# Layer 1 attention: when the row-score products stand among the transposed ones, and where the first row terms are sent

## The reference

```
q = (x @ W_query).reshape(b, n, NUM_HEADS, HEAD_DIM).transpose(0, 2, 1, 3)
k = (x @ W_key).reshape(...)   # v likewise
scores = jnp.einsum('bhqd,bhkd->bhqk', q, k)
scores = jnp.where(causal, -jnp.inf, scores)
attn = jax.nn.softmax(scores / jnp.sqrt(jnp.float32(HEAD_DIM)), axis=-1)
ctx = jnp.einsum('bhqk,bhkd->bhqd', attn, v)
```

## Time and profile before

| | |
|---|---|
| median of three runs | 1362.34 us (1362.08 to 1362.48) |
| profiled execution, its own time | 1362.70 us |
| its span, first to last instruction | 1361.0 us |
| PE busy | 1243.6 us (91%) |
| DVE busy | 812.6 us (60%) |
| ACT busy | 589.7 us (43%) |
| mean granted TensorE clock | 0.962 |
| the stage of layer 1's tiles (first exponential to last) | 808.05 to 1058.64 us |

### The profile page before, as it was taken

One profiled execution on the slowest core, in us unless ns is written; L12 is line 12 of the kernel. 1 busy time (PEld: TensorE's weight loads), 2 busy tenths in 40 slices (PEclk: granted clock), 3 DMA queues, 4 the chain that ended last, 5 costly groups with the idle time before them and its releaser, 6 DMA issues. The chain is left out here.

```text
span 1361.0 us, 18268 instructions
## 1 busy us (share of the span) xinstructions
PE 1243.6 (91%) x5944; PEld 859.5 (63%) x5944; DVE 812.6 (60%) x1732; ACT 589.7 (43%) x1091; POOL 470.8 (35%) x335
## 2 busy tenths in 40 slices
PE   6999999999999999999998968889997478999887
PEld 6866878888887788888885512223322247778665
DVE  6467754444444344444456767777775556878565
ACT  2322633333333333333334425766777153433553
POOL 3101445555555555555563221111111033312000
PEclk9999899999999999999999969999999788999899
DMA  4100253333332643333421350232200301110001
GB/s 152 41 20 1 82 147 109 108 108 108 108 108 54 160 111 108 108 108 108 108 70 47 128 159 22 77 79 70 70 17 17 87 0 47 34 48 24 1 15 47
DMA packets 49308, 102.67 MB, mean 75 GB/s; under 512 B 8660, under 2 KB 21716, under 8 KB 49244
## 3 DMA queue, kind: packets, MB, share of 16 engines
q1 hardware_dynamic: 49244, 101.87, 26.6%
HBM read 88.52 MB, written 8.93 MB: 72 GB/s over the span
## 5 line engine op out<-in xcount | busy, mean ns | idle before, releaser
L473 DVE TENSOR_TENSOR q_t<-q_t,ps 128x512 f32<-128x512 f32 x132 | 90.8, 688 | 230.3 <-ACT q_t L416 227.7
L1554 DVE CUSTOM_DVE_ANT_0 masked<-ps,causal 128x128 f32<-128x128 f32 (+7 forms) x256 | 184.4, 755 | 55.9 <-PE ps L1375 55.1
L529 POOL TENSOR_TENSOR wqkv<-q_t,v_tok 128x512 f32<-128x512 f32 x132 | 198.0, 1516 | 25.9 <-DVE q_t L473 15.2
L519 POOL TENSOR_TENSOR d_w_lo<-raw,d_w_hi 128x768 fp32r<-128x768 f32 x66 | 122.7, 1860 | 242.8 <-ACT d_w_hi L389 242.8
L465 DVE TENSOR_TENSOR wqkv_lo<-wqkv,wqkv_hi 128x512 fp32r<-128x512 f32 x132 | 155.0, 1174 | 67.9 <-ACT wqkv_hi L395 67.9
L311 PE MATMUL ps<-h_hi,d_w_hi 128*128 128x512 f32 x528 | 167.2, 397 | 1.9 <-POOL d_w_lo L519 1.0
L311 PE MATMUL ps<-h_hi,d_w_lo 128*128 128x512 f32 x528 | 166.0, 395 | 0.0
L311 PE MATMUL ps<-h_lo,d_w_hi 128*128 128x512 f32 x528 | 166.0, 395 | 0.0
L1534 ACT ACTIVATE xn<-ps 128x512 f32<-128x512 f32 (+3 forms) x256 | 117.3, 512 | 58.1 <-PE ps L1395 56.3
L389 ACT CAST d_w_hi<-raw 128x768 fp32r<-128x768 f32 x66 | 55.0, 833 | 195.1 <-PE ps L324 193.5
L311 PEld LDWEIGHTS ps<-h_hi,d_w_hi 128*128 128x128 f32 x528 | 98.9, 189 | 25.8 <-POOL d_w_lo L519 1.9
(11 more groups left out here) (252 smaller groups left out, 2119.1 us busy)
## 6 DMA issues: line engine op xcount, KB each, us to landing
v_tok<-router_weights_t SPq DMA_DIRECT2D x132, 256.0 KB, 3.8
raw<-in_moe SPq DMA_DIRECT2D x66, 384.0 KB, 4.3
qk<-qk_parts SPq DMA_DIRECT2D x72, 128.0 KB, 2.7
qk_parts<-parts SPq DMA_DIRECT2D x16, 384.0 KB, 2.7
raw<-in_mlp SPq DMA_DIRECT2D x16, 384.0 KB, 3.1
h_t<-qk_parts SPq DMA_DIRECT2D x24, 128.0 KB, 2.8
x_tok<-in_x SPq DMA_DIRECT2D x4, 512.0 KB, 8.2
h_hi<-raw SPq DMA_DIRECT2D x32, 64.0 KB, 2.3
```

Source lines behind the costliest of these rows:

```text
L473: nc.vector.tensor_tensor(prod[:, s % 3, :], sg[:, s % 3, :], ps[:, 2 * (s % 2) + 1, :], ALU.mult).then_inc(s_t, 1)
L519: nc.gpsimd.tensor_tensor(w_lo[:, slot, :], raw[:, slot, :], w_hi[:, slot, :].bitcast(F32), ALU.subtract).then_inc(s_wlo, 1)
L529: nc.gpsimd.tensor_tensor(inter[:, s % 3, :], prod[:, s % 3, :], wbc[:, s // 2, (s % 2) * GW:(s % 2 + 1) * GW], ALU.mult).then_inc(s_int, 1)
L1554: nc.vector.tensor_tensor_reduce(masked[:, at % 2, 0:k], ps[:, bank:bank + 2, :].rearrange("p a n -> p (a n)")[:, 0:k], causal[:, SEQ - k: ...
```

## The change

Two things are changed; no instruction is added or taken away, and both are changes of order. First, `due` is computed from columns: an item counts its columns and 256 more, a tile likewise, and the list of items is advanced in proportion to the columns of tiles done, between goals at the group ends (R of the group, plus EARLY, plus LEAD). Second, `rows(0)` moves ahead of `load_qk(sp, 2)` and the two loads behind it.

```
-                due = [min(len(entries), ahead + (at * 3 + min(h, 2) + 1) * (HQ * TB + 1) // (3 * NTI)
-                           + min(LEAD, at * LEAD // NTI)) for at in range(NV * NTI) for h in range(HQ)]
+                def columns(n):
+
+                    return (n % TB + 1) * P + 2 * P if n < HQ * TB else 2 * P
+
+                filled = [0] + list(itertools.accumulate(columns(n) for _, n in entries))
+                spent = [0] + list(itertools.accumulate(
+                    (4 * g + 4 - max(4 * g, j)) * P + 2 * P for g, j in tiles for h in range(HQ - 1)))
+
+                def target(v, steps):
+
+                    goal = lambda u, lead: filled[min(len(entries), place[min(u, NV - 1), HQ * TB] + 1 + EARLY + lead)]
+                    a, b = goal(v, LEAD if v else 0), goal(v + 1, LEAD)
+                    return a + (b - a) * spent[steps] // spent[-1]
+
+                due = [sum(c <= target(v, n * (HQ - 1) + min(h, HQ - 2) + 1) for c in filled[1:])
+                       for v in range(NV) for n in range(NTI) for h in range(HQ)]
...
+                        rows(0)
                         sp.wait_ge(s_proj, NJ)
                         load_qk(sp, 2)
...
-                        rows(0)
```

More of the change, by code:

```diff
@@ L3 @@
+import itertools
 from contextlib import ExitStack
```

## The result

The changed kernel takes 1377.24 us (median of 4 runs, 1376.33 to 1378.25) against 1362.41 for the kernel before (4 runs): ratio 1.0096, 95% interval 1.0069 to 1.0122, which is 9.4 to 16.6 us. By the two medians it is slower by 14.8 us, within that interval. The direction was forecast; the size was not: I had written 1368.0 and a range up to 1373.5.

The account below looks back on a forecast made before the run. The stage was taken as bound by engines waiting for one another, none full. The terms -3.3 + 4.0 + 3.3 + 0.6 + 0.3 + 0.8 = +5.7 gave an execution of 1368.4, median 1368.0, range 1362.5 to 1373.5.

Parts of the forecast that it names:

- The start: First row DMA issued ahead of the third group's load, at about 799.8 for 803.10: stage starts 3.3 us earlier.
- my hope of a faster landing with less traffic: From row DMA issue to first tile: less traffic before it could raise the start's gain from 3.3 to 3.9 us.
- The waiting rule: On PE, an item's product starts at the earliest 0.06 us after the scan of the item two before ends.
- the order of a middle group: Groups 1 to 5: waits of 6.2 us against 5.4, so 0.8 more in a group, 4.0 in all.
- The longest step: Step 6 of a middle group: item 2 waits for 8, item 3 behind minus_max; 4.5 to 5 us long.
- steps 5 and 6: Middle group: in step 5 item 7 waits 0.8 us for 5; step 6 lasts 5.0, 2.5 above one without items.
- The clock: PE's half clock: +0.6 us in group 0, +0.8 around the end of group 6, no term for groups 1 to 5.
- the 1.63 of 3.40 us of the earlier trace: PE's busy time from 786.70 to 790.10, before a half clock; used to price +0.8 around group 6's end.
- Group 0: Four more items, 3.3 us of scans on DVE: +3.3 (1.5 to 4.5), with +0.6 for the clock's return.
- Group 6: Waits of 2.2 us for the last R and 2.0 for the row DMA, three items fewer: +0.3 us.
- The range: Execution time with no more than 2 in 10 outside: 1362.5 to 1373.5; upper bound for the groups +9.
- costs twice as much: Rival: minus_max wait reaches step 7, groups 7 and 0 on half clock; +9 for groups, 1373 to 1375; chance 0.1.

Follow-up runs that it names:

- the row DMA alone: Kernel before with only the first row DMA moved ahead of the third group's load: 1361.48 us, ratio 0.9973 to the kernel before.
- the idle products: Changed kernel plus 128x512 products whose result nobody reads, put into PE's waits: 1366.68 us, ratio 1.0014 to the kernel before.
- Two experiments with other orders: Changed kernel with at most one item behind each tile, 1360.63 us; changed kernel with `due` written out by hand by the waiting rule, 1340.34 us.
- the order alone: Changed kernel with `rows(0)` back behind the loads: 1380.17 us, ratio 1.0118 to the kernel before.
- minus_max later: Changed kernel with DVE's four minus_max operations moved behind the scan of the next group's second item (groups 1 to 6): 1366.19 us, ratio 1.0015.
- one item behind a tile: Changed kernel with at most one item behind each tile, the rest going on behind the next tile: 1360.63 us, ratio 0.9983 to the kernel before.
- the four experiments with the same order: Changed kernel with the order alone (1380.17 us), the last group's items early (1373.56), the idle products (1366.68) or minus_max later (1366.19).
- the last group's items early: Changed kernel with group 6's items due no later than in the kernel before: 1373.56 us, ratio 1.0069 to the kernel before.

## Why the prediction was wrong

*The start.* Right: SP's DMA is issued right behind the copy and the first tile comes 2.9 to 3.2 us sooner for 3.3. The way from issue to first tile was 2.97 us and is 3.34 in the changed kernel and 3.03 with the row DMA alone, so my hope of a faster landing with less traffic did not come true.

*The waiting rule and the order of a middle group.* Right. At full clock the group takes 31.95 against 31.28 on average before, +0.67 for the 0.8 of the sum (with the idle products 3.7 us in five groups for 4.0). The longest step was named, its two waits too, and its 4.74 us lie within the 4.5 to 5 that I wrote. Some luck is in the total: steps 5 and 6 came out 0.3 us cheaper each than in my list, and steps 7 and 1, which aren't in it, cost 0.5 and 0.3 (2.99 and 2.24 for the 2.46 and 1.96 of group 7). Two experiments with other orders came out at what the rule gave, 30.38 for 30.4 and 28.73 for 28.5 to 28.8.

*The clock.* This is the step that failed. The sum has the clock at two places: +0.6 in group 0, +0.8 behind group 6, and nothing for groups 1 to 5. I held the 1.63 of 3.40 us of the earlier trace rows against the end of group 6 and not against step 6, where the same sentence of the prediction has PE waiting for half of five microseconds. Measured against the same groups with the idle products, groups 2, 3 and 5 lost 2.4, 1.2 and 1.2 us at half clock, 4.7 in all (34.62, 33.12 and 33.15 for 32.24, 31.96 and 31.96). The sum had nothing there. Group 7 lost 4.6 for 0.8. There I had guessed 3 to 7 us of half clock and it was 20.5; the price was nearly right, 4.6 us for 20.5 where I had 1 to 2 for 3 to 7. The idle products take both losses away (the groups then take 32.24, 31.96, 31.96 and 24.59 us), so this is shown and not only argued. They also exclude DVE's normalization as the cause of group 7's length. Two things stay open. The falls can't be forecast from how busy PE was: 1.64 of 3.40 us was followed by one in group 2 and by none in groups 1 and 4. And it isn't known why the half clock lasted 20.5 us at the end and 6.8 in group 2; behind the same two waits it lasted 23.9 us with the order alone, 13.7 with minus_max later and 10.2 with one item behind a tile.

*Group 0.* Right in kind, short in size: +5.4 for +3.9. Where no later fall of the clock hits it, it takes 40.84 to 42.29 us (the four experiments with the same order), +1.9 to +3.3 where I had +3.3 for the order. In the changed kernel its step 7 took 6.77 us and step 9 5.49, and the clock was halved in both (830.7 to 834.1 and 841.0 to 844.4). With the order alone and with the last group's items early, which change nothing in this group's order, it did not fall there and they took 5.36 and 4.38. So 2.5 us are the clock's, again in a place where the sum had none. My +0.6 was for the clock's return at the start: it came back at 806.8 for 817.4 before, and was then halved once more for 3.4 us.

*Group 6.* +0.8 for +0.3: the two waits were 2.25 and 2.35 us, forecast as 2.2 and 2.0.

*The range.* Its upper end took in 9 us for the groups, but as more waiting. All of the clock's cost together is some 12 us (4.7 + 4.6 + 2.5), where the whole change is +14.3. It stood in the sum with 1.4, and the bounds had at most 2.5 behind group 6. The rival "costs twice as much" (1373 to 1375, chance 0.1) named the half clock in groups 7 and 0 and still came out low.

The Trainium skill (TensorE: Matmul & The Clock Gate, A second HAM failure mode: psum-queue depth-cycling) says that in a kernel which cycles through PSUM banks, short idle moments of PE between groups of matmuls can send its clock back and forth between the two levels. The trace agrees: no gap in the stretch ahead of 899 was above 1.05 us. I had weighed only the long stops.

## What to carry to other kernels

When a change lengthens a wait on PE, ask for each place, and not only the worst one, how busy PE is around it, and compare with a stretch of the same trace behind which the granted clock fell. A place that is as empty may lose the clock in some passes and not in others, so price it as a chance for every group, and look at several groups and runs. Here 1.9 us of waiting in one step cost another 1.2 to 2.5 us where the clock fell, and the two stops of over 2 us in a row 2.0 to 5.6 us of group 7 in four kernels. Spreading work in proportion to its size is right only as far as single items allow: what counted here was whether the item two before was still being scanned, and the proportional table put pairs exactly there. A rule read from a few rows (who waits for which instruction, and for how long after it) that reproduces a middle group's length before to 1% is worth turning round to choose the order: it gave 24 us where the change lost 15.

## What the runs showed of the hardware

- PE's clock fell without any long stop: 1.64 us busy of 3.40, gaps of 1.05 and 0.83 us. With only the first of the two gaps left (minus_max later) it did not fall in any of groups 1 to 5 of the one trace.
- The same emptiness did not always have this effect: 1.64 of 3.40 us in groups 1 and 4 of the changed kernel and 1.36 of 3.40 in group 6 of the kernel before were followed by full clock, 1.32 of 3.40 in group 6 with the last items early by half clock for 3.4 us.
- Groups with the same order of items lost the clock in groups 2, 3 and 5 of the changed kernel, in 1, 2, 3 and 5 with the order alone, in 1, 2, 4 and 5 with the last group's items early, and in none with 7 idle products in the gaps (one trace; the mean granted clock of all ten runs was 0.961 or more).
- Seven idle 128x512 products in 1.9 us of waiting cost nothing (a group at full clock took 31.96 with and 31.95 without); where no wait was, three of them cost 0.54 us a group.
